# The expert stage of an audio tower: three kinds of transposes in one set, a smaller bias product, and two reorderings beside it

## The chip, the cores and the metric

One core of a Trainium2 chip. The metric is the device time of one execution in microseconds (us). The kernel before was timed in three runs: 778.6, 780.52 and 781.25 us, median 780.52. A profiled execution beside them took 779.15 us.

## The reference, cut to what matters

The whole network has three stages on an input of 32 sequences of 250 positions: a token stage (a recurrence), an attention stage, and a mixture of experts. The change is in the third, which is, on h of shape (32, 250, 64):

```python
x = layernorm(h)
gate_logits = x @ gate_w + gate_b                 # 16 experts
topk_vals, topk_idx = top_k(gate_logits, 2)
topk_w = softmax(topk_vals)
h1 = relu(einsum('bsh,ehf->bsef', x, w1) + b1)    # f = 128 for each expert
expert_out = einsum('bsef,efh->bseh', h1, w2) + b2
moe = sum(topk_w * expert_out[topk_idx])
y = x + moe
out = h + (layernorm(y) * gamma + beta)
```

Every expert is computed for every token; the two chosen ones are picked by a weight that is zero for the other 14.

## The kernel before, in words

**Tiling.** Two sequences are one pair of 500 tokens (C), held in four chunks of T = 125 tokens (CH = 4). There are 16 pairs (PAIRS). The 16 experts times 128 hidden units are cut into 16 groups g of 128 rows; each row of a group is one expert e and one of R = 8 residues r, in the order (e, r). For a group, `up` multiplies the tokens by w1 into one bank of PSUM, the hidden rows are passed through relu and multiplied by the routing weights (`gated`), and `down` multiplies by w2 and sums over the groups in banks 0 and 1. Products are 64 x 64 quarters of the array, four at a time: rows 0 to 63 and rows 64 to 127 belong to two groups or two banks.

**Slots.** The stage is a pipeline written out by hand. Each engine runs its own list over p = 1, 2, ...; in p, pair p-1 goes through the experts, pair p is routed, pair p+1 is normalised, and pairs p-2 and p-3 are finished. A p has eight slots v = 0 to 7. In slot v TensorE (`slot_c`, line 1439) does `up` of groups 2v and 2v+1 of pair p-1 (line 1381) and `down` of an earlier slot's groups (line 1403). Below, "up 6" is the `up` of slot 6, and the time of a pair is from its up 0 to the next pair's up 0.

**Banks and waits.** Group g uses bank 4 + g mod 4 (`up_bank`). So `up` of slot v waits (`wait_read`) until groups 2v-4 and 2v-3 have been read. Groups 1, 4, 6, 9, 12 and 14 (`ACT_GROUPS`) are read by ScalarE (relu, line 730) and multiplied by GpSimd (`gate_group`, line 490); the other ten are read and multiplied by VectorE alone (`fused`, line 1029).

**TensorE's other work in a pair:** `logits` (slot 0, line 1412), the token transposes of pair p+1 (`tokens_c`, slot 3, line 1420, into bank 2), the bias product (`extra`, slot 3, line 1390: four products of 250 columns with `b2f`, in which b2 is repeated and divided by R), the transposes of the routing weights of pair p (`weights_c`, slot 6, line 1428, into bank 3) and those of the result of pair p-2 (`fold_c`, slot 6, line 1436).

**VectorE** (`group_c`, line 1080) goes through g = 0 to 15. At each g it does `fused` of group g, and then what `GATE_AT` (line 1078) puts there: the steps n = 0 to 17 of the routing (`gate_step`), a chain of small operations, each on 125 x 64 values or fewer, each waiting for the one before: logits plus bias (line 989), maximum (993), comparisons and products (995, 997, 1001, 1004), difference of the two best (1007), the two weights times their masks (1017, 1018), and their sum, spread over the R = 8 residues (1022, 125 x 512 values). Step 17 (line 1022) stands behind group 8.

**ScalarE** (`slot_c`, line 715): the normalised tokens of pair p+1 (`normed`, line 688) in slot 1, y_low and y_high (the two copies of pair p-2's sums, lines 720 and 722) in slot 3, the copy of the token transposes (line 680) in slot 3, two sigmoids (`gate_weights`) in slot 4, the copy of the weight transposes to wb (line 713) in slot 6, and the relus of its six groups.

**GpSimd** (`step_c`, line 513): the scales of the two layernorms (`c_scales`), then for each of its six groups the product relu x wb, with `c_total` (y_low + y_high, line 496) behind the third of them, group 6, and `c_result` behind groups 9 and 12.

Of the kernel before, what the change touches and what calls it, by code (L numbers as in the profile page):

```python
# [48 lines left out]
C_COLS = C_II + D  # L49


def constants():

    c = np.zeros((128, C_COLS), np.float32)
    c[:, C_IDENT:C_IDENT + 128] = np.eye(128)

    for half in (0, HALF):
        for part in range(1, PARTS):
            rows = slice(half + part, half + XROWS, PARTS)
            for r in (rows, half + XROWS + part):  # L60
                c[r, C_W1] = -1.0
                c[r, C_W2] = -1.0 if part == 2 else 0.0
    c[64:, C_MS1] = -1.0
    c[Q_ROW + H:Q_ROW + 2 * H, C_MS2] = -1.0
    c[K_ROW + H:K_ROW + 2 * H, C_MS2] = -1.0
    c[:, C_II:C_II + D] = np.tile(np.eye(D), (2, 1))
    for h in range(H):
        c[K_ROW + h, C_IND + h] = 1.0
        c[K_ROW + H + h, C_IND + h] = 1.0
    return c  # L70


def build(nc, cst, xin, xparts, acws, w24, wqT, wkT, wvT, woT, wq, wk, gam, lns,
          gw, gb, w1, b1, w2, b2, fg, fb, out):
    with ExitStack() as ctx:
# [20 lines left out]
        b2raw, b2f = sb("b2raw", [128, D]), sb("b2f", [128, D])  # L96
        fg_sb, fb_sb = sb("fg_sb", [T, D]), sb("fb_sb", [T, D])
# [28 lines left out]
        wtok = sb("wtok", [T, CH, E, R])  # L126
# [45 lines left out]
        s_wprod = sem("s_wprod")  # L172
        a_xin, a_split, a_scr, a_table = sem("a_xin"), sem("a_split"), sem("a_scr"), sem("a_table")
# [91 lines left out]
        def up_bank(g):  # L265
            return bank[4 + g % 4]

# [71 lines left out]
        def _(gp):  # L339
# [173 lines left out]
            def step_c(p):  # L513
                if p < PAIRS + 2:
                    c_scales(p + 1)
                if p == PAIRS:
                    gp.wait_ge(b_res, PAIRS)
                    gp.tensor_tensor(h_fb[:, :, :], h_all[:, (PAIRS - 1) * CH:PAIRS * CH, :],
                                     fb_sb[:, :].unsqueeze(1).to_broadcast([T, CH, D]), ALU.add).then_inc(c_hfb, 1)
                for n, g in enumerate(ACT_GROUPS):  # L520
                    if valid(p - 1):
                        gate_group(p - 1, g)
                    if n == 2 and 0 <= p - 2 < PAIRS - 1:
                        c_total(p - 2)
# [10 lines left out]
        def _(act):  # L535
# [120 lines left out]
            def start_c(v):  # L656

                if v == 0:
                    normed(0)
# [18 lines left out]
            def tokens_c(q):  # L678
                act.wait_ge(c_xt, q + 1)
                act.activation(cs1[q % 3][:, :], bank[2][:, 0:C], ACT.Copy).then_inc(c_s1, 1)  # L680
# [28 lines left out]
            def token_weights(p):  # L709
                act.wait_ge(c_wt, p + 1)  # L710
                wait(act, c_gated, (G - len(ACT_GROUPS)) * (p - 1))
                wait(act, c_gatep, len(ACT_GROUPS) * (p - 1))
                act.activation(wb[p % 2][:, :], bank[3][:, 0:C], ACT.Copy).then_inc(c_wbs, 1)

            def slot_c(p, v):
# [7 lines left out]
                if v == 4 and valid(p):  # L723
                    gate_weights(p)
                for g in (2 * v, 2 * v + 1):
# [6 lines left out]
                if v == 1 and valid(p + 1):  # L732
                    normed(p + 1)
                if v == 5 and 0 <= p - 3 < PAIRS - 1:
                    result(p - 3)
                if v == 3 and valid(p + 1):
                    tokens_c(p + 1)
                if v == 6 and valid(p):
                    token_weights(p)

# [7 lines left out]
        def _(dve):  # L748
# [224 lines left out]
            def gate_step(p, n):  # L973
# [104 lines left out]
            GATE_AT = {2: (0,), 3: (1, 2, 3), 4: (4, 5, 6), 5: (7, 8, 9), 6: (10, 11), 7: (12, 16), 8: (17,)}  # L1078
# [35 lines left out]
        def _(pe):  # L1114
# [234 lines left out]
            def start_c(v):  # L1349

                if v == 1:
                    pe.wait_ge(b_ev, 16 * PAIRS)
                    pe.wait_ge(b_gl, 4 * PAIRS)
                    tokens_c(0)
# [18 lines left out]
            def up(q, v):  # L1373
# [33 lines left out]
            def logits(p):  # L1407
                pe.wait_ge(c_s1, p + 1)
                wait(pe, c_wbs, p)
# [6 lines left out]
            def tokens_c(q):  # L1416
                pe.wait_ge(c_hn, q + 1)
                wait(pe, c_yt, q - 3)
                for c in range(CH):
                    last = pe.transpose(bank[2][:, c * T:(c + 1) * T],  # L1420
# [3 lines left out]
            def weights_c(p):  # L1424
                pe.wait_ge(c_gate, gate_count(p, GATE))
                wait(pe, c_wbs, p)
                for c in range(CH):
                    last = pe.transpose(bank[3][:, c * T:(c + 1) * T],  # L1428
                                        wtok[:, c, :, :].rearrange("p e r -> p (e r)"), ident[0:T, 0:T])
# [9 lines left out]
            def slot_c(p, v):  # L1439
# [104 lines left out]
```

## Time and profile before

| | |
|---|---|
| timed runs | 778.6 to 781.25 us, median 780.52 |
| the profiled execution | 779.15 us, its span 776.6 us |
| TensorE | busy 740.7 us (95% of the span) |
| VectorE | busy 623.8 us (80%) |
| ScalarE | busy 531.5 us (68%) |
| GpSimd | busy 459.4 us (59%) |
| granted TensorE clock | 0.994 of full speed |
| expert stage | from about 498 us to the end |

The expert stage takes about 278 us of the span. Each pair in its middle takes the same time to 0.02 us. The page of the profile gives busy times over the whole span, so the stage has to be read by stretches, and its order by the timeline of each engine.

### The profile page before, as it was taken

The page shows a single profiled execution, that of the slowest core. Times are in us where ns is not written, and L with a number is a line of the kernel's source. Part 1 is how long each engine was busy: PE and PEld are TensorE (multiplying, and loading weights), DVE is VectorE, ACT ScalarE, POOL GpSimd, SP SyncE. Part 2 cuts the span into 40 slices and gives each one's busy share as a digit, 9 for nine tenths or more (in the row PEclk, how much of TensorE's full clock was granted, in tenths as well). Part 3 has the DMA queues.
Part 4 walks back from the last instruction along what each step waited for, and adds up shares of the span by engine and source line. Part 5 has one row for each costly group of instructions (what it writes and reads, how often), then busy time and mean ns, then how long its engine had stood idle before and what let it go on. Part 6 is the DMA issues. An engine that isn't in the chain of part 4 may idle for free.

```text
span 776.6 us, 16767 instructions
## 1 busy us (share of the span) xinstructions
PE 740.7 (95%) x5712; PEld 434.7 (56%) x5712; DVE 623.8 (80%) x1534; ACT 531.5 (68%) x1053; POOL 459.4 (59%) x620
## 2 busy tenths in 40 slices
PE   2999999999999999999999999999999999999994
PEld 1444356676667666676666766444555555454431
DVE  7676777888878888788878887788888888888864
ACT  1566779888888889888898888654555655545441
POOL 7654324654456444564446541366788787888885
PEclk9999999999999999999999999999999999999997
DMA  6300202111221112211221112000000000000000
GB/s 188 94 2 2 55 1 56 35 38 40 55 56 28 42 42 56 53 31 34 51 56 34 37 41 54 2 2 1 9 15 8 9 8 8 9 16 7 9 7 20
DMA packets 22619, 25.46 MB, mean 33 GB/s; under 512 B 12520, under 2 KB 21480, under 8 KB 22408
## 3 DMA queue, kind: packets, MB, share of 16 engines
q1 hardware_dynamic: 21544, 23.14, 12.8%
q10 hardware_dynamic: 992, 1.26, 0.6%
q8 instruction: 46, 0.75, 0.4%
q14 instruction: 37, 0.30, 0.1%
HBM read 5.06 MB, written 2.43 MB: 10 GB/s over the span
## 4 chain that ended last, share of the span: by engine, by line
PE 75%; DVE 10%; DMA 4%; POOL 4%; ACT 3%; issue 3%; SPq 1%; ACTq 0%; DVEq 0%; POOLq 0%
PE bank L1403 14%; PE bank L1381 13%; PE bank L1274 11%; PE bank L1232 9%; PE bank L1298 7%; PE bank L1145 5%; PE bank L1300 5%; DVE m L863 3%; DVE prob L909 3%; DMA m<-s2o 2%; DMA m<-s2e 2%; PE bank L1135 2%; SPq L319 1%; PE bank L1428 1%; PE bank L1236 1%
## 5 line engine op out<-in xcount | busy, mean ns | idle before, releaser
L444 POOL TENSOR_TENSOR sq<-sq 125x256 f32<-125x256 f32 x128 | 98.0, 777 | 187.1 <-ACT sq L596 164.4
L909 DVE TENSOR_SCALAR prob<-prob,cap_hi,cap_lo 125x500 f32<-125x500 f32 x256 | 149.1, 610 | 41.7 <-ACT prob L632 38.7
L632 ACT ACTIVATE prob<-bank 125x500 f32<-125x500 f32 x256 | 148.4, 591 | 33.9 <-PE bank L1300 31.6
L1381 PE MATMUL bank<-cs,w_sb 64*64 64x500 f32 x1024 | 147.0, 580 | 2.2 <-DVE gated L1029 2.0
L1403 PE MATMUL bank<-gated,w_sb 64*64 64x500 f32 x1024 | 148.8, 588 | 0.0
L490 POOL TENSOR_TENSOR gated<-relu,wb 128x500 f32<-128x500 f32 x96 | 120.0, 1251 | 48.1 <-ACT relu L730 45.6
L1029 DVE SCALAR_TENSOR_TENSOR gated<-bank,nb,wb 128x500 f32<-128x500 f32 x160 | 114.8, 727 | 35.2 <-PE bank L1381 35.2
L730 ACT ACTIVATE relu<-bank,b_sb 128x500 f32<-128x500 f32 x96 | 64.7, 674 | 93.2 <-PE bank L1381 93.2
L1381 PEld LDWEIGHTS bank<-cs,w_sb 64*64 64x64 f32 x1024 | 53.1, 133 | 54.7 <-issue 48.1
L596 ACT ACTIVATE sq<-bank 125x512 f32<-125x512 f32 x128 | 75.3, 600 | 4.8 <-POOL sq L444 1.6
L1232 PE MATMUL bank<-wqku_hi,s 128*125 128x512 f32 x192 | 77.2, 402 | 0.0
L1232 PE MATMUL bank<-wqku_lo,s 128*125 128x512 f32 x192 | 75.7, 394 | 0.0
L1403 PEld LDWEIGHTS bank<-gated,w_sb 64*64 64x64 f32 x1024 | 47.0, 132 | 45.0 <-issue 38.3
L1274 PE MATMUL bank<-prob,ue 125*64 125x250 f32 x512 | 61.0, 380 | 0.0
L1274 PE MATMUL bank<-prob,uo 125*64 125x250 f32 x512 | 61.0, 380 | 0.0
L1298 PE MATMUL bank<-m1o,s 128*125 128x500 f32 x128 | 55.4, 433 | 3.3 <-DMA m<-s2o 2.3
L1145 PE MATMUL bank<-st_a,w_sb 64*64 64x500 f32 x224 | 57.8, 588 | 0.0
L1298 PE MATMUL bank<-m1e,s 128*125 128x500 f32 x128 | 55.2, 431 | 2.6 <-DMA m<-s2e 1.6
L1145 PE MATMUL bank<-st_b,w_sb 64*64 64x500 f32 x224 | 57.3, 588 | 0.0
L553 ACT ACTIVATE st_a<-bank 128x500 f32<-128x500 f32 x56 | 32.2, 589 | 32.7 <-PE bank L1145 22.7
L801 DVE TENSOR_SCALAR st_b<-bank 128x500 f32<-128x500 f32 x56 | 37.3, 677 | 20.3 <-PE bank L1145 19.7
L863 DVE TENSOR_TENSOR m<-bank,m1o 64x500 fp32r<-64x500 f32 x64 | 43.2, 675 | 12.5 <-ACT m1o L591 11.8
(188 smaller groups left out, 1572.7 us busy)
## 6 DMA issues: line engine op xcount, KB each, us to landing
m1e<-m1e SPq DMA_DIRECT2D x64, 125.0 KB, 2.3
m1o<-m1o SPq DMA_DIRECT2D x64, 125.0 KB, 2.3
out<-res SPq DMA_DIRECT2D x15, 125.0 KB
w_sb<-in_w SPq DMA_DIRECT2D x1, 1024.0 KB
xa<-xparts SPq DMA_DIRECT2D x3, 281.2 KB
w_sb<-in_w SPq DMA_DIRECT2D x1, 512.0 KB
xw<-xparts SPq DMA_DIRECT2D x3, 140.6 KB
xparts<-x_part SPq DMA_DIRECT2D x3, 125.0 KB, 3.5
```

Of the source, the lines that this page charges most:

```text
L444: gp.tensor_tensor(sq2[q][:, :, :], sq[q][:, :, 0:D // 2], sq[q][:, :, D // 2:D], ALU.add)\
L490: gp.tensor_tensor(gated[g % 8][:, :], relu_sb[n % 3][:, :], wb[q % 2][:, :], ALU.mult).then_inc(c_gatep, 1)
L596: act.activation(sq[k % 2][:, :, :], src[0:T, :].rearrange("p (h d) -> p h d", h=H), ACT.Square)\
L632: act.activation(prob[v % PROBS][:, :, c, :], bank[5 + n % 3][0:T, 0:C].rearrange("p (h l) -> p h l", h=2), ACT.Exp).then_inc(b_exp, 1)
L909: dve.tensor_scalar(part, part, cap_hi[0:T, h:h + 1], cap_lo[0:T, h:h + 1], ALU.min, ALU.max)\
L1029: dve.scalar_tensor_tensor(gated[g % 8][:, :], up_bank(g)[:, 0:C], nb1[:, g:g + 1], wb[q % 2][:, :], ALU.max, ALU.mult).then_inc(c_gated, 1)
L1145: last = pe.matmul(dst[cols, 0:C].rearrange("p (b l) -> p b l", b=2), w24_sb[rows, 0, :], src[rows, :, 0:L], start=False, stop=True)
L1232: last = pe.matmul(dst[0:T, :], s1[j][:, c * T:(c + 1) * T], w[:, q, :], start=first, stop=not first)
L1274: last = pe.matmul(bank[1][64 * c:64 * c + 64, 0:L], u_sb[jj][:, 2 * b + c, h * D:(h + 1) * D], prob[v % PROBS][:, hh, c, :], start=h == 0 ...
L1298: pe.matmul(ps, s1[o][:, cols], m1[o][:, 2 * hp:2 * hp + 2, b * L:(b + 1) * L], start=True, stop=False)
L1381: last = pe.matmul(up_bank(g)[cols, 0:C], w1_sb[rows, g, cols], cs1[q % 3][rows, :], start=True, stop=True)
L1403: last = pe.matmul(y[cols, 0:C], w2_sb[rows, g, :], gated[g % 8][rows, :], start=v == 0, stop=v == 7, skip_group_check=True)
```

## The change

- **One set.** `tokens_c(p+1)` moves from TensorE's slot 3 to slot 6, between `weights_c(p)` and `fold_c(p-2)`. On ScalarE the copy of the tokens follows from slot 3 to slot 6.
- **Banks.** The weight transposes go to bank 6, which is the `up` bank of groups 10 and 14, and wait until group 10 has been read; `up` of slot 7 waits until they have been copied. The token transposes go to bank 3.
- **Step 17 of the routing** (line 1022) moves from behind group 8 to behind step 16, ahead of `fused` of group 8. The sum is laid out as (r, e) in place of (e, r), and w1, b1, w2 are reordered on the host to match.
- **Bias product.** b2 is summed over the residues once (one small product into bank 4 and one copy, in the last attention step), so that each of the four products needs only its own 125 tokens.
- **Two orders.** `normed(p+1)` moves on ScalarE from slot 1 to slot 4, behind the sigmoids and ahead of the relu of group 9. `c_total` moves on GpSimd from behind group 6 to behind group 9.

```diff
-C_COLS = C_II + D
+C_SUM = C_II + D
+C_COLS = C_SUM + 128
...
+    for half in (0, HALF):
+        c[:, C_SUM + half:C_SUM + half + E] = np.tile(np.eye(E), (R, 1))
...
+        def tokens_bank(q):
+            return bank[2 if q < 2 else 3]
+
+        def weights_bank(p):
+            return bank[3] if p == 0 else up_bank(14)
...
-                    if n == 2 and 0 <= p - 2 < PAIRS - 1:
+                    if n == 3 and 0 <= p - 2 < PAIRS - 1:
                         c_total(p - 2)
...
+                if v == 2:
+                    act.wait_ge(c_bsum, 1)
+                    act.activation(b2s[:, :], bank[4][:, 0:D], ACT.Copy).then_inc(c_bias, 1)
...
                 if v == 4 and valid(p):
                     gate_weights(p)
+                if v == 4 and valid(p + 1):
+                    normed(p + 1)
                 for g in (2 * v, 2 * v + 1):
...
-                if v == 1 and valid(p + 1):
-                    normed(p + 1)
...
-                if v == 3 and valid(p + 1):
-                    tokens_c(p + 1)
                 if v == 6 and valid(p):
                     token_weights(p)
+                if v == 6 and valid(p + 1):
+                    tokens_c(p + 1)
...
-                    first, second = (lg[:, k, :, :].unsqueeze(3).to_broadcast([T, CH, E, R]) for k in (5, 6))
+                    first, second = (lg[:, k, :, :].unsqueeze(2).to_broadcast([T, CH, R, E]) for k in (5, 6))
...
-            GATE_AT = {2: (0,), 3: (1, 2, 3), 4: (4, 5, 6), 5: (7, 8, 9), 6: (10, 11), 7: (12, 16), 8: (17,)}
+            GATE_AT = {2: (0,), 3: (1, 2, 3), 4: (4, 5, 6), 5: (7, 8, 9), 6: (10, 11), 7: (12, 16, 17)}
...
+                    pe.matmul(bank[4][:, 0:D], c_sb[:, C_SUM:C_SUM + 128], b2f[:, :], start=True, stop=True)\
+                        .then_inc(c_bsum, 1)
...
+                if v == 7 and valid(q + 1):
+                    pe.wait_ge(c_wbs, q + 2)
...
-                for cols, part in ((LO, slice(0, L)), (HI, slice(L, C))):
-                    for rows, y in ((LO, bank[0]), (HI, bank[1])):
-                        pe.matmul(y[cols, part], b2f[rows, :], wb[q % 2][rows, part], start=False, stop=False,
-                                  skip_group_check=True)
+                for c, (cols, rows, y) in enumerate(((LO, LO, bank[0]), (HI, LO, bank[0]), (LO, HI, bank[1]), (HI, HI, bank[1]))):
+                    part = slice(c * T, (c + 1) * T)
+                    pe.matmul(y[cols, part], b2s[rows, :], wb[q % 2][rows, part], start=False, stop=False,
+                              skip_group_check=True)
...
             def tokens_c(q):
                 pe.wait_ge(c_hn, q + 1)
-                wait(pe, c_yt, q - 3)
+                if q >= 2:
+                    pe.wait_ge(c_gate, gate_count(q - 1, 1))
...
             def weights_c(p):
                 pe.wait_ge(c_gate, gate_count(p, GATE))
                 wait(pe, c_wbs, p)
+                if p > 0:
+                    wait_read(pe, p - 1, 10)
...
             def fold_c(q):
                 pe.wait_ge(c_y, q + 1)
-                pe.wait_ge(c_s1, min(q + 4, PAIRS))
+                pe.wait_ge(c_s1, 2)
+                wait(pe, c_yt, q)
...
-                if v == 3:
-                    if valid(p + 1):
-                        tokens_c(p + 1)
                 if v == 6:
                     if valid(p):
                         weights_c(p)
+                    if valid(p + 1):
+                        tokens_c(p + 1)
                     if valid(p - 2):
                         fold_c(p - 2)
```

## Rows read from the trace of the kernel before

**Rows 1.** Stretches: length, busy PE, PEld, DVE, ACT, POOL, granted clock, DMA, GB/s
```profile
548.00:713.00 165.00, 164.98 (x1644) 83.26 (x1640) 144.39 (x438) 88.89 (x200) 133.97 (x141) 1.00 0.04 10
```

**Rows 2.** Timeline of TensorE, one pair (start us, us, engine, line, operation)
```profile
596.69 1.02 PE L1381 MATMUL bank<-cs,w_sb 64*64 64x500 f32 x8
...
602.10 1.08 PE L1381 MATMUL bank<-cs,w_sb 64*64 64x500 f32 x8
603.11 0.65 PE L1420 MATMUL bank<-c_sb,cxn 125*128 125x125 f32 x4
603.69 1.40 PE L1403 MATMUL bank<-gated,w_sb 64*64 64x500 f32 x8
...
608.35 1.34 PE L1381 MATMUL bank<-cs,w_sb 64*64 64x500 f32 x8
...
613.21 1.02 PE L1381 MATMUL bank<-cs,w_sb 64*64 64x500 f32 x8
```

**Rows 3.** Timeline of VectorE, the same pair
```profile
599.92 0.74 DVE L1029 SCALAR_TENSOR_TENSOR gated<-bank,nb,wb 128x500 f32<-128x500 f32 x1 [1.08 <-PE bank L1381]
...
601.60 0.50 DVE L995 TENSOR_TENSOR lg<-lg,top 125x64 f32<-125x64 f32 x1
...
602.64 0.22 DVE L1001 TENSOR_TENSOR lg<-lg,top 125x64 f32<-125x64 f32 x1
...
603.93 0.45 DVE L1007 TENSOR_TENSOR top<-top 125x4 f32<-125x4 f32 x1
...
606.00 1.17 DVE L1017 TENSOR_TENSOR lg<-lg,top 125x64 f32<-125x64 f32 x1
...
607.23 0.73 DVE L1029 SCALAR_TENSOR_TENSOR gated<-bank,nb,wb 128x500 f32<-128x500 f32 x1
607.88 1.08 DVE L1022 TENSOR_TENSOR wtok<-lg 125x512 f32<-125x512 f32 x1
```

**Rows 4.** Timeline of GpSimd, the same pair
```profile
603.11 1.25 POOL L490 TENSOR_TENSOR gated<-relu,wb 128x500 f32<-128x500 f32 x1 [1.10 <-ACT relu L730]
...
605.85 1.24 POOL L496 TENSOR_TENSOR y_moe<-y_low,y_high 128x500 f32<-128x500 f32 x1
```

**Rows 5.** Timeline of ScalarE, the same pair
```profile
600.83 1.65 ACT L688 ACTIVATE cxn<-h_all,cnb,cinv 125x128 f32<-125x128 f32 x4 [2.37 <-POOL cnb L482]
```

**Rows 6.** Timeline of VectorE in p = 15, which normalises no further pair
```profile
732.29 0.74 DVE L1029 SCALAR_TENSOR_TENSOR gated<-bank,nb,wb 128x500 f32<-128x500 f32 x1 [1.07 <-PE bank L1381]
...
734.94 1.10 DVE L1001 TENSOR_TENSOR lg<-lg,top 125x64 f32<-125x64 f32 x1
...
737.95 1.16 DVE L997 TENSOR_TENSOR lg<-lg,desc 125x64 f32<-125x64 f32 x1
...
739.92 0.46 DVE L1001 TENSOR_TENSOR lg<-lg,top 125x64 f32<-125x64 f32 x1
740.41 0.77 DVE L1017 TENSOR_TENSOR lg<-lg,top 125x64 f32<-125x64 f32 x1
...
741.89 0.68 DVE L1022 TENSOR_TENSOR wtok<-lg 125x512 f32<-125x512 f32 x1
```

**Rows 7.** Timeline of GpSimd in p = 15
```profile
734.72 1.24 POOL L490 TENSOR_TENSOR gated<-relu,wb 128x500 f32<-128x500 f32 x1 [0.40 <-ACT relu L730]
...
737.71 1.31 POOL L496 TENSOR_TENSOR y_moe<-y_low,y_high 128x500 f32<-128x500 f32 x1
```

**Rows 8.** Timeline of TensorE in p = 15
```profile
729.06 1.02 PE L1381 MATMUL bank<-cs,w_sb 64*64 64x500 f32 x8
...
740.15 1.07 PE L1381 MATMUL bank<-cs,w_sb 64*64 64x500 f32 x8 [1.08 <-DVE gated L1029]
...
742.02 1.07 PE L1381 MATMUL bank<-cs,w_sb 64*64 64x500 f32 x8
...
746.60 1.02 PE L1381 MATMUL bank<-cs,w_sb 64*64 64x500 f32 x8
```

**Rows 9.** DMA issues of the first 30 us: KB, us to landing
```profile
c_sb<-in_cst ACTq DMA_DIRECT2D x1, 102.0 KB, 3.2
```

More of the change, by code:

```diff
@@ L96, in build @@
         b2raw, b2f = sb("b2raw", [128, D]), sb("b2f", [128, D])
+        b2s = sb("b2s", [128, D])
         fg_sb, fb_sb = sb("fg_sb", [T, D]), sb("fb_sb", [T, D])
@@ L125, in build @@
         desc = sb("desc", [T, E])
-        wtok = sb("wtok", [T, CH, E, R])
+        wtok = sb("wtok", [T, CH, R, E])
         cagg, cvar = sb("cagg", [T, 2, CH, 2]), sb("cvar", [T, 2, CH])
@@ L172, in build @@
         s_wprod = sem("s_wprod")
+        c_bsum, c_bias = sem("c_bsum"), sem("c_bias")
         a_xin, a_split, a_scr, a_table = sem("a_xin"), sem("a_split"), sem("a_scr"), sem("a_table")
@@ L679, in tokens_c @@
                 act.wait_ge(c_xt, q + 1)
-                act.activation(cs1[q % 3][:, :], bank[2][:, 0:C], ACT.Copy).then_inc(c_s1, 1)
+                act.activation(cs1[q % 3][:, :], tokens_bank(q)[:, 0:C], ACT.Copy).then_inc(c_s1, 1)
             def normed(q):
@@ L712, in token_weights @@
                 wait(act, c_gatep, len(ACT_GROUPS) * (p - 1))
-                act.activation(wb[p % 2][:, :], bank[3][:, 0:C], ACT.Copy).then_inc(c_wbs, 1)
+                act.activation(wb[p % 2][:, :], weights_bank(p)[:, 0:C], ACT.Copy).then_inc(c_wbs, 1)
             def slot_c(p, v):
@@ L1353, in start_c @@
                     pe.wait_ge(b_gl, 4 * PAIRS)
+                    pe.matmul(bank[4][:, 0:D], c_sb[:, C_SUM:C_SUM + 128], b2f[:, :], start=True, stop=True)\
+                        .then_inc(c_bsum, 1)
+                    pe.wait_ge(b_gl, 4 * PAIRS)
                     tokens_c(0)
@@ L1387, in extra @@
                 pe.wait_ge(c_wbs, q + 1)
-                for cols, part in ((LO, slice(0, L)), (HI, slice(L, C))):
-                    for rows, y in ((LO, bank[0]), (HI, bank[1])):
-                        pe.matmul(y[cols, part], b2f[rows, :], wb[q % 2][rows, part], start=False, stop=False,
-                                  skip_group_check=True)
+                if q == 0:
+                    pe.wait_ge(c_bias, 1)
+                for c, (cols, rows, y) in enumerate(((LO, LO, bank[0]), (HI, LO, bank[0]), (LO, HI, bank[1]), (HI, HI, bank[1]))):
+                    part = slice(c * T, (c + 1) * T)
+                    pe.matmul(y[cols, part], b2s[rows, :], wb[q % 2][rows, part], start=False, stop=False,
+                              skip_group_check=True)
             def down(q, v):
@@ L1408, in logits @@
                 pe.wait_ge(c_s1, p + 1)
-                wait(pe, c_wbs, p)
+                if p == 1:
+                    pe.wait_ge(c_wbs, 1)
                 for c in range(CH):
@@ L1417, in tokens_c @@
                 pe.wait_ge(c_hn, q + 1)
-                wait(pe, c_yt, q - 3)
+                if q >= 2:
+                    pe.wait_ge(c_gate, gate_count(q - 1, 1))
                 for c in range(CH):
-                    last = pe.transpose(bank[2][:, c * T:(c + 1) * T],
+                    last = pe.transpose(tokens_bank(q)[:, c * T:(c + 1) * T],
                                         cxn[q % 4][:, c, :, :].rearrange("p a d -> p (a d)"), ident[0:T, 0:T])
@@ L1426, in weights_c @@
                 wait(pe, c_wbs, p)
+                if p > 0:
+                    wait_read(pe, p - 1, 10)
                 for c in range(CH):
-                    last = pe.transpose(bank[3][:, c * T:(c + 1) * T],
-                                        wtok[:, c, :, :].rearrange("p e r -> p (e r)"), ident[0:T, 0:T])
+                    last = pe.transpose(weights_bank(p)[:, c * T:(c + 1) * T],
+                                        wtok[:, c, :, :].rearrange("p r e -> p (r e)"), ident[0:T, 0:T])
                 last.then_inc(c_wt, 1)
@@ L1508 @@
     oT = a("L0_attn_W_o").reshape(D, H, D).transpose(2, 1, 0)
-    w1 = a("L0_ffn_w1").reshape(E, D, G, R)
+    w1 = a("L0_ffn_w1").reshape(E, D, G, R).transpose(1, 2, 3, 0).reshape(D, G, 128)
     arrays = {
@@ L1525 @@
         "gb": rows(a("L0_ffn_gate_b"), T),
-        "w1": np.tile(w1.transpose(1, 2, 0, 3).reshape(D, G, 128), (2, 1, 1)),
-        "b1": a("L0_ffn_b1").reshape(E, G, R).transpose(0, 2, 1).reshape(128, G),
-        "w2": a("L0_ffn_w2").reshape(E, G, R, D).transpose(0, 2, 1, 3).reshape(128, G, D),
-        "b2": np.repeat(a("L0_ffn_b2"), R, axis=0),
+        "w1": np.tile(w1, (2, 1, 1)),
+        "b1": a("L0_ffn_b1").reshape(E, G, R).transpose(2, 0, 1).reshape(128, G),
+        "w2": a("L0_ffn_w2").reshape(E, G, R, D).transpose(2, 0, 1, 3).reshape(128, G, D),
+        "b2": np.tile(a("L0_ffn_b2"), (R, 1)),
         "fg": rows(a("L0_ffn_gamma"), T),
```

## The prediction

> **What bounds the kernel now.** I read the stage by stretches first. In the middle of the expert stage TensorE is busy 164.98 of 165 us at full granted clock [rows 1], while VectorE has 144.39. So TensorE sets the pace there, and one pair takes 613.21 - 596.69 = 16.52 us [rows 2]. The chain of waits says the same: it runs through TensorE for the whole stretch. Next I asked how near the other engines are, because the change rearranges all of them. The reader should look for the point at which TensorE needs something of VectorE. That is up 6, at 608.35 [rows 2], which overwrites the banks of groups 8 and 9 and needs `fused` of group 8 done. VectorE's list from `fused` of group 2 (it starts at 599.92, having waited 1.08 for TensorE) to the end of `fused` of group 8 (607.23 + 0.73 = 607.96) is 8.04 us without a gap [rows 3]. It is done 0.39 before up 6. So there is a second loop, hidden under TensorE by only 0.39 us a pair: VectorE's list from group 2 to group 8, then TensorE from up 6 to the next pair's up 1, which releases the next group 2.
>
> **What makes VectorE's list long.** Some small operations take far longer than their size. L1017 has 125x64 values and takes 1.17, and L1001 of the same size takes 0.22 [rows 3]. L1017 starts at 606.00 and ends at 607.17, and GpSimd's y_moe runs from 605.85 to 607.09 [rows 4]. L1007 (0.45) ends at 604.38, GpSimd's product of group 4 at 604.36. An operation of VectorE with two inputs in SBUF thus stands still until the GpSimd instruction that began before it has ended; `fused`, which reads PSUM, does not (607.23 takes its usual 0.73). The Trainium skill, SBUF — State Buffer, section "Who interferes with whom", states this as an exclusive lock for such pairs, held by whoever issues first; the trace agrees with it, L1017 ending 0.08 after y_moe. So it matters which of the two begins first, and the change moves both.
>
> **The pair in which the new order can be seen.** In p = 15 there is no further pair to normalise and no tokens to transpose in slot 3. In the changed kernel `normed` is gone from slot 1 and the tokens from slot 3 in every p. What ScalarE does there now is 1.65 us of `normed` at 600.83, waiting for GpSimd's scales, with the relu of group 4 queued behind it [rows 5]; GpSimd's product of group 4 then starts 603.11 - 596.69 = 6.42 after up 0 [rows 4], when L1001 (602.64, that is 5.95) is through [rows 3]. In p = 15 the relu is not held, the product starts 734.72 - 729.06 = 5.66 after up 0 [rows 7], 0.22 ahead of L1001 (734.94, that is 5.88), and L1001 takes 1.10 [rows 6]. TensorE stands 1.08 us for `fused` of group 7 at 740.15, and the pair takes 746.60 - 729.06 = 17.54 [rows 8], though it has less work.
>
> **The change part by part.**
> - *One set.* From up 3 (602.10) to the next product (603.69) are 1.59 us [rows 2]. Less the 0.84 of an `up` (16 of them and the smaller work make a pair) and an estimated 0.45 for four transposes (above 0.58, the 603.11 to 603.69 of them, it can't be; below a third of the 0.65 shown it hardly is), 0.30 is the change of the array from quarters to the whole and back, saved once a pair. The transposes themselves are not saved: their 0.45 moves to slot 6.
> - *Bias product.* A group's 500 columns take 0.84, so 250 take 0.42 and 125 take 0.21: saved between 0 (if the number of instructions, which stays, were the limit) and 0.21; I take 0.21.
> - These two are worth 0.51 a pair if TensorE stays the bound. They lie between up 3 and up 4, which is outside TensorE's part of the second loop. If that loop is the bound they save nothing.
> - *Step 17 ahead of group 8* puts L1022 into the second loop: 0.68 unheld [rows 6], 1.08 held [rows 3]. It now stands at the point where GpSimd is idle, waiting for the relu of group 9, which `normed` (1.65) holds back. I take 0.68; bounds 0.68 and 0.68 + 1.24. The other layout of its sum has as many values and costs nothing.
> - *`normed` to slot 4.* It waits for nothing there. Queued behind it are the relu of group 9 (needed by up 6 and by down 4), the relu of group 12 and the copies of slot 6. The relu of group 9 comes some 11.1 after up 0 and up 6 later, so nothing, unless VectorE's list gets short. Its leaving slot 1 is what releases the relu of group 4.
> - *`c_total` behind group 9.* y_moe then no longer stands in front of L1017 (0.95 saved against today) or L997. The fold needs it; it ends near 13.6 and the fold starts near 13.8. Nothing, with little to spare.
> - *Weights by way of bank 6.* They wait for group 10, which VectorE has two operations after group 8, while up 6 runs (0.84): nothing. Up 7 waits for the copy wb; two more sets of transposes and a `down` lie between (1.8 us), against 0.6 for the copy: nothing.
> - *At the ends.* One small product and one copy, once, in attention's last step: 0.1. Constants are 128 columns longer than the 102 KB that land in 3.2 [rows 9], under GpSimd's clearing of memory: 0, above 0.3 without that cover.
>
> **The sum.** VectorE's list as in p = 15: from 732.29 to 0.08 after L1022's start, where `fused` of group 8 ends (as 607.96 to 607.88): 741.97, that is 9.68. Three of its holds go, since y_moe and group 9 now come later: L997 1.16 to 0.22 (y_moe at 737.71 [rows 7]), L1001 0.46 to 0.22, L1017 0.77 to 0.22: 1.73 less. L1022 comes in: 0.68 more. That is 8.63, against 8.04 today. Then 0.10 until up 6 starts (it started 0.05 after), 746.60 - 742.02 = 4.58 to the next up 0 [rows 8], 0.45 for the tokens now in that set, and 3.23 from up 0 to `fused` of group 2 (599.92 - 596.69, and 732.29 - 729.06). Sum 16.99, against 16.52 now: 0.47 more a pair. TensorE's own work would be 16.52 - 0.51 = 16.01; it waits about 1 us a pair.
> Thirteen pairs (p = 2 to 14): +6.1. p = 1 has the same list with more of the routing of its own: between 0 and +0.9, I take +0.5. In p = 15 no `normed` holds back the relu of group 9, so group 9 and y_moe fall on L1001 and L1017 ahead of up 6: 8.63 + 0.95 + 0.95, and L1018 about 0.5 more, is 11.0 against 9.68: +1.4, bounds -0.9 (no hold) and +1.9. p = 16: -0.2. Ends +0.1. Together +7.9: the profiled execution's 779.15 becomes 787.0, and the median, which was 1.4 above it, 788.4. Errors of 0.3 a pair either way give 784 to 793.
>
> **The rivals.**
> *TensorE stays the bound (faster).* The place is GpSimd's group 4 against L1001. If the product starts after L1001, its 0.88 is gone, L1007 comes ahead of group 6, and the list is at most 7.7; TensorE holds the pace once it is under 16.01 - 0.10 - 4.58 - 0.45 - 3.23 = 7.65. Then 14 pairs save 0.51, p = 15 falls from 17.54 by some 1.9: 780.5 - 7.1 - 1.9 - 0.2, about 771. For it speaks a margin of only 0.22 us; against it, that p = 15 shows this order with the same work ahead of it. The Trainium skill, TensorEngine Tiling (Array Packing), section "Key Properties", says that a change of tiling mode drains TensorE, so fewer changes must pay; the rows give 0.30 each, and that decides nothing while VectorE is the bound. Chance 0.12.
> *No difference.* The list comes to 8.16, where the loop is 16.52: half of the holds fall out. 778.2 to 782.8. Chance 0.06.
> *More holds.* The product of group 9 gets ahead of L1022, or L1017, in every pair: that takes 0.65 us of a margin, and costs another 1 us in 13 pairs: about 801. Chance 0.06.
> *The bias product does not shrink.* It changes nothing in the forecast and 3 us in the first rival.
>
> **How the numbers follow.** The forecast has 0.76 and its own range is 784 to 793. Down to 780 it takes in the case without difference and partial holds; the far cases, 771 and 801, are left out, less than 2 in 10 with it. 0.3% (2.3 us) is about what a measurement of this kernel can tell from no change. Faster 0.13, within it 0.05, slower 0.82.
>
> **What would show it.** In the profile after: a pair of 16.9 to 17.1 with L1001 near 0.9 to 1.1 at its first place and L1007 near 0.7; L1017 and L1022 at 0.21 and 0.68; TensorE waiting for `fused` before up 4, up 5 and up 6, about 1 us in all, where it waited for nothing; one set of 12 transposes; the bias product at half its time. It is wrong if L1001 keeps its 0.22, or if TensorE has no idle time in the middle of the stage.

## The result, and the profile after

The changed kernel takes 788.89 us (median of five runs, 787.37 to 789.38) against 780.52 before: the ratio is 1.0103, with a 95% interval of 1.0089 to 1.0116. The forecast was 788.4. The profiled execution took 787.37 us, its span is 785.0 (before: 776.6). Two executions in the experiments below (934 and 1485 us, of the two kernels with two sets, whose other executions lie between 776 and 784) are far off the rest, and the ratios leave them out.

Where the 8.4 us lie can be read from the starts of `logits`, one per pair (worked out from the timeline of TensorE):

| part of the span, us | before | after | difference | forecast |
|---|---|---|---|---|
| start to the first `logits` | 484.63 | 485.34 | +0.7 | +0.1 |
| p = 0 | 14.95 | 14.94 | 0 | 0 |
| p = 1 | 15.58 | 16.07 | +0.5 | +0.5 |
| p = 2 to 14, thirteen pairs | 214.73 | 220.67 | +5.9 | +6.1 |
| p = 15 to the end | 46.66 | 47.93 | +1.3 | +1.2 |

The line numbers have moved: `up` is now L1400, `down` L1424, the bias product L1411, `fused` L1043, the product of GpSimd L501, y_moe L507; the steps L1001, L1007, L1017 and L1022 are L1015, L1021, L1031 and L1036.

First the stretch of [rows 1] in the changed kernel, same columns:

```profile
548.00:713.00 165.00, 162.93 (x1604) 72.96 (x1600) 136.32 (x427) 86.95 (x193) 125.65 (x137) 1.00 0.04 10
```

TensorE still looks full: 162.93 of 165 us. The idle 2.07 us would be 0.2 us in each of the stretch's 9.7 pairs, though a pair is 0.44 us longer with less work in it. Ends of matmuls are modelled, so a short wait between two groups hardly shows in a busy share. The starts show it. One pair of TensorE, to set beside [rows 2]:

```profile
600.39 1.02 PE L1400 MATMUL bank<-cs,w_sb 64*64 64x500 f32 x8
...
605.80 1.08 PE L1400 MATMUL bank<-cs,w_sb 64*64 64x500 f32 x8
606.86 1.44 PE L1424 MATMUL bank<-gated,w_sb 64*64 64x500 f32 x7
...
608.43 1.07 PE L1400 MATMUL bank<-cs,w_sb 64*64 64x500 f32 x8
609.29 1.05 PE L1424 MATMUL bank<-gated,w_sb 64*64 64x500 f32 x8
610.55 1.07 PE L1400 MATMUL bank<-cs,w_sb 64*64 64x500 f32 x8 [0.21 <-DVE gated L1043]
...
612.35 1.07 PE L1400 MATMUL bank<-cs,w_sb 64*64 64x500 f32 x8
...
617.36 1.02 PE L1400 MATMUL bank<-cs,w_sb 64*64 64x500 f32 x8
```

The pair takes 617.36 - 600.39 = 16.97. Up 5 (610.55) starts 2.12 after up 4, where an `up` and a `down` are 1.68; up 6 (612.35) starts 1.80 after up 5; up 4 starts 1.57 after down 0 (606.86), where a `down` and the smaller bias product are 1.05. That is 1.08 us of gaps, all before the three `up`s that were named. The bracket shows 0.21 of it. They cost 0.71 net: the pair takes 16.26 in the version below in which VectorE is out of the way. The other 0.37 is lost in that version too, in another form. The half of down 0 that writes bank 1 starts 0.39 behind the half that writes bank 0. With gaps the late half catches up in them; without, it stays late until the transposes (down 0 to up 6 takes 4.66 there, where the products are 4.41, and up 6 to the transposes 1.12 in place of 1.00).

VectorE and GpSimd in the same pair, to set beside [rows 3, 4]:

```profile
603.62 0.74 DVE L1043 SCALAR_TENSOR_TENSOR gated<-bank,nb,wb 128x500 f32<-128x500 f32 x1 [1.07 <-PE bank L1400]
...
606.33 1.05 DVE L1015 TENSOR_TENSOR lg<-lg,top 125x64 f32<-125x64 f32 x1
...
608.44 0.66 DVE L1021 TENSOR_TENSOR top<-top 125x4 f32<-125x4 f32 x1
...
610.56 0.22 DVE L1031 TENSOR_TENSOR lg<-lg,top 125x64 f32<-125x64 f32 x1
...
610.96 0.69 DVE L1036 TENSOR_TENSOR wtok<-lg 125x512 f32<-125x512 f32 x1
611.57 2.02 DVE L1043 SCALAR_TENSOR_TENSOR gated<-bank,nb,wb 128x500 f32<-128x500 f32 x3
...
606.05 1.25 POOL L501 TENSOR_TENSOR gated<-relu,wb 128x500 f32<-128x500 f32 x1 [0.35 <-ACT relu L746]
607.84 1.25 POOL L501 TENSOR_TENSOR gated<-relu,wb 128x500 f32<-128x500 f32 x1 [0.55 <-ACT relu L746]
611.62 1.25 POOL L501 TENSOR_TENSOR gated<-relu,wb 128x500 f32<-128x500 f32 x1 [2.53 <-ACT relu L746]
```

GpSimd's product of group 4 begins at 606.05, 0.28 ahead of L1015, and L1015 ends 0.08 after it (606.33 + 1.05 against 606.05 + 1.25). L1021 runs against group 6 (607.84). L1031 and L1036 are free, because group 9 comes at 611.62 and y_moe behind it. From `fused` of group 2 to the end of `fused` of group 8 (611.57 + 0.73) are 8.68 us.

### The profile page after: what moved, and what is told of

It is laid out like the page before. It is cut to its first block, busy times and chain, and to the rows that moved or that the text cites. A ratio compares the mean times of both kernels' runs of the same rounds, so it can differ in the third digit from the quotient of the medians.

```text
span 785.0 us, 16762 instructions
## 1 busy us (share of the span) xinstructions
PE 744.7 (95%) x5714; PEld 425.2 (54%) x5714; DVE 620.0 (79%) x1534; ACT 533.5 (68%) x1054; POOL 453.8 (58%) x620
## 4 chain that ended last, share of the span: by engine, by line
PE 62%; DVE 20%; DMA 6%; issue 5%; ACT 3%; POOL 3%; SPq 1%; ACTq 0%; DVEq 0%; POOLq 0%
PE bank L1288 11%; PE bank L1400 9%; PE bank L1246 9%; PE bank L1312 7%; PE bank L1424 7%; PE bank L1159 5%; PE bank L1314 5%; DVE gated L1043 4%; DVE m L877 3%; DVE prob L923 3%; DMA m<-s2o 2%; DVE lg L1015 2%; DMA m<-s2e 2%; PE bank L1149 2%; SPq L330 1%
## 5 line engine op out<-in xcount | busy, mean ns | idle before, releaser
L501 POOL TENSOR_TENSOR gated<-relu,wb 128x500 f32<-128x500 f32 x96 | 119.7, 1249 | 62.2 <-ACT relu L746 61.4
L1043 DVE SCALAR_TENSOR_TENSOR gated<-bank,nb,wb 128x500 f32<-128x500 f32 x160 | 113.8, 728 | 46.1 <-PE bank L1400 46.1
L1400 PE MATMUL bank<-cs,w_sb 64*64 64x500 f32 x1024 | 136.6, 588 | 6.9 <-DVE gated L1043 6.7
L1424 PE MATMUL bank<-gated,w_sb 64*64 64x500 f32 x1024 | 141.9, 587 | 0.2
L1400 PEld LDWEIGHTS bank<-cs,w_sb 64*64 64x64 f32 x1024 | 41.8, 132 | 69.3 <-issue 50.8
L1424 PEld LDWEIGHTS bank<-gated,w_sb 64*64 64x64 f32 x1024 | 44.7, 132 | 55.8 <-issue 48.0
```

The lines of the kernel that those rows point to most:

```text
L501: gp.tensor_tensor(gated[g % 8][:, :], relu_sb[n % 3][:, :], wb[q % 2][:, :], ALU.mult).then_inc(c_gatep, 1)
L1043: dve.scalar_tensor_tensor(gated[g % 8][:, :], up_bank(g)[:, 0:C], nb1[:, g:g + 1], wb[q % 2][:, :], ALU.max, ALU.mult).then_inc(c_gated, 1)
L1400: last = pe.matmul(up_bank(g)[cols, 0:C], w1_sb[rows, g, cols], cs1[q % 3][rows, :], start=True, stop=True)
L1424: last = pe.matmul(y[cols, 0:C], w2_sb[rows, g, :], gated[g % 8][rows, :], start=v == 0, stop=v == 7, skip_group_check=True)
```

## Experiments

Each is the changed kernel with one edit, unless it says otherwise. A *hold* is the time by which an operation of VectorE with two inputs in SBUF takes longer than usual because a GpSimd instruction that began before it has not ended. The ratio is to the kernel before on the same chip, with its 95% interval; "pair" is the steady distance from one `logits` to the next in the middle of the stage (16.53 before, 16.97 changed).

### Which of the reorderings costs what

**`normed` back to slot 1.**

```diff
-                if v == 4 and valid(p + 1):
-                    normed(p + 1)
...
+                if v == 1 and valid(p + 1):
+                    normed(p + 1)
```

> The changed kernel (788.9 us) with normed back in ScalarE's slot 1, all else kept. Theory A (the pair's time is VectorE's list from group 2 to group 8, and which GpSimd product stands in front of its two-input operations sets that list): the relu of group 4 is held back again, so the first L1015 goes back from 1.05 to 0.22 us; but the relu of group 9 is no longer behind normed, its product begins about 2 us earlier and falls in front of the routing's last steps (L1031, L1036). Laid out with the durations of the trace: a pair of 16.75 in place of 16.97, in all about 2 us less: 787. Rival B (the set of three in slot 6, with weights waiting for group 10 and up 7 for the copy wb, is what makes the pair longer): nothing on that path moves, 16.97 a pair, 789, and the first L1015 does not matter.

Measured: 786.92 us, ratio 1.0067 [1.0043, 1.0091], pair 16.75. The product of group 4 now starts after the first L1015, which falls to 0.22, as the forecast's cause requires. But only 0.22 of the 0.44 us comes back. The expectation had the number, but not the reason: it let the product of group 9 fall on L1031 and L1036, and the product begins at 610.42, when L1036 (609.85, 0.69) has begun and runs free. VectorE's list ends at 611.19, 0.35 ahead of up 6 (611.54), so it no longer sets the pace. A second bound lies right under the first: down 0 waits for y_low, which stands on ScalarE behind `normed` and the relu of group 4. It is read below beside the kernel with two sets.

**`c_total` back behind group 6** (`n == 3` to `n == 2`).

> The changed kernel with c_total (y_moe) back behind GpSimd's group 6. Theory A: y_moe then runs directly behind the product of group 6, in front of L1011 and the steps after it, and everything behind comes under the product of group 9 as well: a pair of about 18.8 in place of 16.97, some 24 us more in all: 813. Rival B (set of three is the cause): y_moe is ready 2 us earlier for the fold, so no change or a gain of up to 0.1 a pair: 787 to 789.

Measured: 812.82 us, ratio 1.0396 [1.0369, 1.0423], pair 18.83. Timeline of VectorE and GpSimd, one pair:

```profile
617.59 1.15 DVE L1011 TENSOR_TENSOR lg<-lg,desc 125x64 f32<-125x64 f32 x1
...
620.20 1.62 DVE L1036 TENSOR_TENSOR wtok<-lg 125x512 f32<-125x512 f32 x1
...
617.36 1.30 POOL L507 TENSOR_TENSOR y_moe<-y_low,y_high 128x500 f32<-128x500 f32 x1
619.93 1.34 POOL L501 TENSOR_TENSOR gated<-relu,wb 128x500 f32<-128x500 f32 x1 [1.28 <-ACT relu L746]
```

y_moe holds L1011 (1.15 for 0.23), that makes VectorE late, and so the product of group 9 now begins 0.27 ahead of L1036 (1.62 for 0.69). Two holds of 0.92 and 0.93 are the whole 1.86 us a pair. One hold breeds the next: this is the largest effect in the study, and no engine has more work.

**Step 17 back behind group 8.**

```diff
-            ... 7: (12, 16, 17)}
+            ... 7: (12, 16), 8: (17,)}
```

> The changed kernel with step 17 (L1036) back behind fused of group 8, as before the change. Theory A with the holds laid out: behind group 8 the step begins only after the product of group 9 has begun and is held by it to its end (about 1.1 to 1.3 in place of 0.69), group 10 is late, and the transposes wait for the step: about 17.3 a pair, 793. Theory A in the simple form of the prediction's sum (0.68 us of VectorE's list is taken out of the loop, and nothing else moves): 16.97 - 0.6 = 16.4 a pair, 781. Rival B: 789 or more, as weights come later.

Measured: 791.37 us, ratio 1.0131 [1.0109, 1.0154], pair 17.36. Step 17 is off VectorE's list before up 6, and still the pair is 0.39 longer. Timeline of VectorE, GpSimd and TensorE, one pair:

```profile
614.16 0.68 DVE L1036 TENSOR_TENSOR wtok<-lg 125x512 f32<-125x512 f32 x1
...
614.29 1.67 POOL L501 TENSOR_TENSOR gated<-relu,wb 128x500 f32<-128x500 f32 x1 [2.53 <-ACT relu L746]
...
617.23 0.70 PE L1462 MATMUL bank<-c_sb,y_moe 128*125 128x128 f32 x4 [0.26 <-POOL y_moe L507]
```

The expectation had the size, but let GpSimd hold VectorE. It is the other way round. VectorE begins first and GpSimd is held: the product of group 9 takes 1.67 instead of 1.25, y_moe behind it is late by as much, and TensorE's fold waits for y_moe. So the moves of step 17 and of `c_total` belong together. With `c_total` behind group 9, GpSimd's order is on the path too.

### The bias product

**The bias product of before, 4 x 250 columns with b2f, in the changed kernel.**

> The changed kernel with the old bias product (four products of 250 columns with b2f). Theory A: it lies between up 3 and up 4, where TensorE waits for fused of group 5 anyway, so 0.0 a pair: 788.9, and TensorE's wait in front of up 4 is 0.2 shorter. Rival C (TensorE's own work still counts in the pair): 0.21 more in each of 16 pairs, 3.3 us: 792.

Measured: 789.02 us, ratio 1.0104 [1.0078, 1.0131], pair 16.97: no difference. The smaller product is worth nothing here.

**The bias product alone, on the kernel before** (with the (r, e) layout that it needs; one set, `normed`, `c_total` and step 17 as before).

> The kernel before (780.6 us, 16.53 a pair) with nothing of the change but the smaller bias product and the (r, e) layout that it needs. Theory C (TensorE is the bound before, 164.98 of 165 us busy, so work taken from it is gained): 0.21 less in 16 pairs, 3.3 us: 777. Theory A (the holds decide, and VectorE's list has only 0.39 us of slack): up 4 and everything behind it comes 0.2 earlier, so the relu and the GpSimd product of group 6 and of group 9 come earlier against VectorE's steps, and steps that were just ahead of them fall under them. Laid out: about 17.0 a pair, 785; with latencies off by 0.02 us it can stay at 16.5 (779), so 779 to 786, and no gain of 3 us.

Measured: 785.58 us, ratio 1.0069 [1.0052, 1.0085], pair 16.98. Work was taken from an engine that was busy 164.98 of 165 us, and the kernel became slower by 0.45 us a pair. The two timelines side by side, VectorE and GpSimd. Before:

```profile
607.09 0.21 DVE L1018 TENSOR_TENSOR lg<-lg,top 125x64 f32<-125x64 f32 x1
...
607.16 1.25 POOL L490 TENSOR_TENSOR gated<-relu,wb 128x500 f32<-128x500 f32 x1
```

With the bias product alone:

```profile
609.40 1.17 DVE L1025 TENSOR_TENSOR lg<-lg,top 125x64 f32<-125x64 f32 x1
610.49 1.28 DVE L1026 TENSOR_TENSOR lg<-lg,top 125x64 f32<-125x64 f32 x1
...
609.25 1.24 POOL L501 TENSOR_TENSOR y_moe<-y_low,y_high 128x500 f32<-128x500 f32 x1
610.45 1.24 POOL L495 TENSOR_TENSOR gated<-relu,wb 128x500 f32<-128x500 f32 x1
```

Before, VectorE's second product (L1018) begins 0.07 us ahead of GpSimd's group 9, which was still waiting for its relu. With TensorE 0.21 us earlier the relu is ready, the product follows y_moe at once, begins 0.04 ahead of L1026, and L1026 takes 1.28 instead of 0.21. That is theory A of the expectation, also in its number. The kernel before was held together by a margin of 0.07 us that no view of busy shares shows.

**Two sets as before, with the smaller bias product, `c_total` behind group 9 and step 17 ahead of group 8** (on the kernel before). This is the changed kernel without the one set and without the move of `normed`.

> The kernel that stands to e1_normed_slot1 (786.9, 16.75 a pair) as two sets to one: token transposes in slot 3 into bank 2, weight transposes in bank 3, their copy in slot 3; all else as in e1 (smaller bias product, step 17 ahead of group 8, c_total behind group 9, normed in slot 1). Theory F (in slot 3 the token transposes cover the time in which down 0 would otherwise wait for ScalarE's y_low and y_high, and their 0.45 us is not in the part of the loop behind up 6): one set costs, it does not save: two sets give 16.37 a pair, and in all about 780. Theory G (what the change says: one change of the array's mode less per pair is gained when the rest is equal): two sets cost 0.3 a pair more than one: 17.05, 791.

Measured: 781.31 us, ratio 1.0009 [0.9994, 1.0023], pair 16.32. That is 16.53 - 0.21: TensorE is the bound again, with exactly the bias product's saving. Against the first experiment (pair 16.75), which differs by the one set alone, the one set costs 0.43 us a pair. Timeline of TensorE with one set (first experiment):

```profile
605.56 1.08 PE L1400 MATMUL bank<-cs,w_sb 64*64 64x500 f32 x8
607.11 1.44 PE L1424 MATMUL bank<-gated,w_sb 64*64 64x500 f32 x8 [0.47 <-ACT y_low L734]
...
611.54 1.41 PE L1400 MATMUL bank<-cs,w_sb 64*64 64x500 f32 x8
...
614.32 1.07 PE L1424 MATMUL bank<-gated,w_sb 64*64 64x500 f32 x8
```

and with two:

```profile
602.44 1.08 PE L1391 MATMUL bank<-cs,w_sb 64*64 64x500 f32 x8
...
604.03 1.39 PE L1415 MATMUL bank<-gated,w_sb 64*64 64x500 f32 x8
...
608.49 1.34 PE L1391 MATMUL bank<-cs,w_sb 64*64 64x500 f32 x8
...
610.78 1.07 PE L1415 MATMUL bank<-gated,w_sb 64*64 64x500 f32 x8
```

From up 3 to down 0 are 1.55 us with one set and 1.59 with two. The transposes are gone from there, but down 0 overwrites banks 0 and 1 and must wait for the copies y_low and y_high; the transposes had filled exactly that wait. From up 6 to down 3 are 2.78 with one set and 2.29 with two: the tokens' 0.49 is really added there. In sum +0.45 by these rows (0.43 by the pairs), and nothing of the change of the array is saved.

The same parts of the span as in the table above, worked out for this kernel, show why it doesn't beat the one before although each of its pairs does: thirteen pairs give 2.7 us, p = 1 takes back 1.0 and p = 15 to the end 2.7. In p = 15 no `normed` delays the relu of group 9, and its product and y_moe hold VectorE in turn. Some 1.5 us of the last 2.7 are of another kind. TensorE stands still for VectorE ahead of up 6 of p = 15:

```profile
742.11 1.94 PE L1391 MATMUL bank<-cs,w_sb 64*64 64x500 f32 x8 [2.31 <-DVE gated L1037]
```

Up 6 takes 1.94 us where it takes 1.07 in the changed kernel (750.57, shown further down, after as long a wait), and up 6 to the next up 0 takes 6.08 against 4.58. The granted clock is 0.50 from 742 to 744 us here (1.2 of 2.4 GHz) and 1.00 throughout p = 15 in the changed kernel. The first experiment's trace has the same fall (granted clock 0.65 from 748 to 750 us and 0.50 from 750 to 752), with p = 15 to the end at 49.5. A wait of 2.3 us in this place was followed by half clock in two of the five traces that have it. The timed executions of this kernel point the same way: with a mean granted clock of 0.995 they took 778.2 to 779.7 us (three), with 0.992 or 0.993 they took 780.2 to 783.3 (eight). By an estimate from the three, this kernel takes 0.5 to 2 us less than the one before where the clock stays up.

### What the hold is made of

**Step 5 with its second input from PSUM** (it reads bank 3 instead of the maxima in SBUF; the token transposes wait for it).

> The changed kernel with step 5 of the routing (the first L1015 of a pair, 1.05 us) taking its second input from PSUM (the logits' bank) in place of SBUF, same size and same place, and the token transposes waiting for it. The comparison then has another right side, so the mask of the best expert, and with it the weights and the output, are not the reference's; the work is the same in amount. Theory A (a VectorE operation with two SBUF inputs stands still under a GpSimd instruction that began first): step 5 takes 0.2 us though the product of group 4 runs at that moment; the next two-input steps and the relu of group 9 move 0.8 earlier and meet the products of groups 6 and 9 instead, so the pair gains little: 16.9 to 17.0, 788 to 789. Rival D (the step is slow for its data or its wait, not for GpSimd): it stays near 1.05. Rival E (holds add up): the pair falls by the whole 0.8: 16.2, 777.

Measured: 786.62 us, ratio 1.0081 [1.0063, 1.01], pair 16.98. Timeline, one pair:

```profile
605.08 0.22 DVE L1015 TENSOR_TENSOR lg<-lg,bank 125x64 f32<-125x64 f32 x1
605.33 0.80 DVE L1021 SCALAR_TENSOR_TENSOR lg<-lg 125x64 f32<-125x64 f32 x1
...
604.80 1.25 POOL L501 TENSOR_TENSOR gated<-relu,wb 128x500 f32<-128x500 f32 x1 [0.35 <-ACT relu L746]
```

With one input from PSUM the same step takes 0.22 in the middle of GpSimd's product, where it took 1.05. So it is the second SBUF input that is held, not the operation. The next step, which has two, then stands until the product's end (0.80, ending 0.08 after it). The hold moves by one instruction, and the pair stays as it is. The time that is gained lies in p = 1, where 15.04 us stand for 16.07.

**The steps of the routing spread ahead of the products.**

```diff
-            GATE_AT = {2: (0,), 3: (1, 2, 3), 4: (4, 5, 6), 5: (7, 8, 9), 6: (10, 11), 7: (12, 16, 17)}
+            GATE_AT = {1: (0, 1, 2, 3), 4: (4, 5), 5: (6,), 6: (7, 8, 9), 7: (10, 11, 12, 16, 17)}
```

> The changed kernel with GATE_AT = {1: (0, 1, 2, 3), 4: (4, 5), 5: (6,), 6: (7, 8, 9), 7: (10, 11, 12, 16, 17)}: four steps are moved ahead of fused of group 2, into the 1.07 us in which VectorE waits for up 1 there. Simple count of VectorE's list: about 1 us shorter, a pair of 16.0, 774. Theory A with the holds laid out: step 2 then meets the 1.66 us power of c_scales on GpSimd (L491, from 2.16 to 3.82 after up 0) and is held until it ends, so fused of group 2 is late: about 17.2 a pair, 791.

Measured: 775.33 us, ratio 0.9942 [0.9923, 0.9962], pair 16.26. Theory A's expectation failed, in sign and by 16 us; the simple count's 774 is near. Timeline of VectorE, GpSimd and TensorE, one pair:

```profile
598.63 0.23 DVE L1009 TENSOR_TENSOR lg<-lg,top 125x64 f32<-125x64 f32 x1
598.89 0.22 DVE L1011 TENSOR_TENSOR lg<-lg,desc 125x64 f32<-125x64 f32 x1
...
598.22 1.66 POOL L491 TENSOR_TENSOR cinv<-cvar,mhalf 125x8 f32<-125x8 f32 x1
...
601.47 1.08 PE L1400 MATMUL bank<-cs,w_sb 64*64 64x500 f32 x8
602.53 1.44 PE L1424 MATMUL bank<-gated,w_sb 64*64 64x500 f32 x7
```

Steps 2 and 3 have two inputs in SBUF and run inside GpSimd's L491 (the power of `c_scales`, 1.66 us on 125x8 values), and neither is held. All 28 such overlaps of steps 2 and 3 in this trace are at 0.22 or 0.23. The expectation had let L491 hold them to its end. VectorE's list from group 2 to group 8 is 7.85 us after that (599.28 to 607.13), in place of 8.68. By the sum of the forecast its loop would take 7.85 + 0.05 + 5.01 + 3.23 = 16.14, less than the 16.26 measured, so VectorE no longer sets the pace, though by only 0.12. The same stretch of the profile shows:

```profile
548.00:713.00 165.00, 165.00 (x1680) 86.01 (x1678) 144.41 (x453) 91.00 (x201) 135.34 (x144) 1.00 0.05 10
```

**The same with `c_scales` behind GpSimd's group 1.**

> As the run before, with c_scales moved on GpSimd behind the product of group 1, so that VectorE's four steps do not meet its 1.66 us power. Theory A with the holds laid out: the steps run while VectorE would wait for up 1, the list from group 2 to 8 fits under TensorE nearly everywhere, 16.2 a pair in place of 16.53 before and 16.97 after: about 775, faster than both. Rival B (set of three is the cause): no gain against after: 789.

Measured: 775.86 us, ratio 0.9946 [0.993, 0.9963], pair 16.26. As L491 holds nothing, moving it gains nothing. One of the thirteen pairs takes 17.29 here, and it shows what a margin is. In the others L1036 begins 0.05 or 0.06 us ahead of GpSimd's product of group 9 and is free (0.69). In this one VectorE is 0.17 us late for a reason that the trace doesn't show, the product begins first (655.28 against 655.39), and L1036 takes 1.68.

**Two sets with the steps moved ahead** (the kernel with two sets above, with this order of the steps).

```diff
+            GATE_AT = {1: (0,), 2: (1,), 3: (2, 3, 4), 4: (5, 6), 5: (7,), 7: (8, 9, 10, 11, 12, 16), 8: (17,)}
```

> As s1_two_sets, with GATE_AT = {1: (0,), 2: (1,), 3: (2, 3, 4), 4: (5, 6), 5: (7,), 7: (8, 9, 10, 11, 12, 16), 8: (17,)}: one step in the wait ahead of group 2, and the two-input steps gathered where GpSimd's products leave room. Theory A with the holds laid out: 16.45 a pair, p = 15 without its 1 us of waiting: 775 to 777, which would make the single set unnecessary for the best time. If the set of three is worth something by itself, this stays above g1_steps_ahead_only (775.3) by more than 3 us: 778 or more.

Measured: 778.1 us, ratio 0.9968 [0.9955, 0.9981], pair 16.44. The pair is as expected (16.45), the time is above the 775 to 777 named. It lies 2.8 us above the one set with the steps spread, just under the 3 that were to tell whether the one set is worth something by itself, and the two differ in the order of the steps too: that stays open. Inside the stage it is 2.9 us shorter than before, 1.3 of it in the thirteen pairs and 1.6 from p = 15 on. Its pair is 0.12 longer than with two sets and the first order of steps: step 17 behind group 8 stretches y_moe from 1.24 to 1.71 (610.19 to 611.90), and the fold starts right behind it, at 611.95.

The fastest version of the study is thus the changed kernel with the steps spread: 775.33 us, 0.58% under the kernel before and 1.7% under the changed one.

## Why the prediction was right

**The loop.** The forecast's sum held term by term: list 8.68 (forecast 8.63), 0.05 until up 6 (0.10), 5.01 from up 6 to the next up 0 (4.58 + 0.45), 3.23 to `fused` of group 2 (3.23): 16.97 against 16.99. The signs that it named are there: 1.05 at the first L1015, 0.66 at L1021, 0.22 and 0.69 at L1031 and L1036, waits before up 4, 5 and 6. Of the 1.08 us of gaps (forecast about 1) only 0.71 count, since TensorE's own pair is 16.26. What made this possible was p = 15 of the kernel before [rows 6 to 8], which showed the new order of events in the old trace.

**p = 1 and p = 15.** The +0.5 of p = 1 is as forecast, but it was the middle of a range from 0 to 0.9, with nothing laid out behind it: luck. p = 15 takes 18.97 us from up 0 to up 0 (forecast 17.54 + 1.4). Timeline of TensorE, VectorE and GpSimd, to set beside [rows 6 to 8]:

```profile
736.18 1.02 PE L1400 MATMUL bank<-cs,w_sb 64*64 64x500 f32 x8
...
750.57 1.07 PE L1400 MATMUL bank<-cs,w_sb 64*64 64x500 f32 x8 [2.31 <-DVE gated L1043]
...
755.15 1.02 PE L1400 MATMUL bank<-cs,w_sb 64*64 64x500 f32 x8
...
746.36 1.16 DVE L1031 TENSOR_TENSOR lg<-lg,top 125x64 f32<-125x64 f32 x1
747.45 1.27 DVE L1032 TENSOR_TENSOR lg<-lg,top 125x64 f32<-125x64 f32 x1
748.75 1.11 DVE L1036 TENSOR_TENSOR wtok<-lg 125x512 f32<-125x512 f32 x1
...
746.11 1.33 POOL L501 TENSOR_TENSOR gated<-relu,wb 128x500 f32<-128x500 f32 x1 [1.23 <-ACT relu L746]
```

The size is right and the places are one later than forecast: group 9, y_moe and the operation behind them fall on L1031, L1032 and L1036 (0.94, 1.05 and 0.42 too long), not on the second L1001 and L1017. (The lower bound given for p = 15, -0.9, should be -1.05 by its own sum, 8.63 against 9.68; nothing rests on it.)

**Ahead of the stage.** Here a term was mis-sized: "ends +0.1" against +0.7. But the change is not what did it. The 0.7 arises near 21 us, where one stretch of the recurrence's products still ran at nearly half the speed; from 22 us on the changed kernel's recurrence is 0.73 behind throughout. TensorE of before and then of after:

```profile
20.76 0.58 PE L1145 MATMUL bank<-st_a,w_sb 64*64 64x500 f32 x1
```

```profile
20.89 1.04 PE L1159 MATMUL bank<-st_b,w_sb 64*64 64x500 f32 x2
```

The first `logits` start between 484.22 and 487.18 us in the twelve profiled executions, and at 484.22 and 484.63 in two that have the same constants and first products as the changed kernel. In the traces of before and of the `c_total` experiment 8 of these products take about 1.04 us, in the changed kernel 16. So this part differs by up to 3 us from one execution to the next, and that the total came within 0.5 us of the forecast is in part chance. The granted clock of the stretch from 20 to 22 us is 1.00 in both traces; what slows the products there is open. Inside the stage the forecast was +7.8 and the measurement +7.7.

**TensorE's own work was too low.** The forecast gave 16.01 us a pair and, in the first rival, 771 us, if VectorE had been fast enough. With VectorE out of the way the pair takes 16.26, not 16.01. The step that failed is the saving of "One set": it counted the change of the array (0.30) as pure gain and took the tokens out of slot 3 at no cost, but they covered down 0's wait for ScalarE's copies. ScalarE in the changed kernel:

```profile
606.13 0.59 ACT L734 ACTIVATE y_low<-bank 128x500 f32<-128x500 f32 x1 [0.16 <-PE bank L1424]
```

It starts as soon as the sums are there and its end, 606.72, is what releases the first half of down 0 at 606.86. Up 3 to down 0 is 1.06 where an `up` is 0.84: 0.22 us of waiting. The half of down 0 that writes bank 1 waits for y_high, the next copy:

```profile
606.61 0.58 ACT L736 ACTIVATE y_high<-bank 128x500 f32<-128x500 f32 x1
```

In every trace, before the change too, that half starts 0.05 us after y_high has ended; it is the 0.39 behind the first half that was named above. So TensorE waited for ScalarE in the kernel before as well, under a busy share of 164.98 of 165. With `normed` in slot 1 the copies are later still, and the same wait is 0.71. The forecast's number didn't depend on it, since VectorE's list was longer; the rival's 771 did.

The Trainium skill, TensorEngine Tiling (Array Packing), section "Key Properties", says that a change of mode drains TensorE. The one set of the changed kernel agrees: up 6 to down 3 takes 2.44 us, and less the 0.84 of an `up` and three times the 0.43 of four transposes (613.83 to 614.26) that leaves 0.31 for the way out and back. The forecast's 0.30 was thus right in size, but the row that it was read from doesn't show it: up 3 to down 0 takes 1.59 with the transposes and 1.55 without. One such way less was worth 0.06 us a pair at best (16.32 with two sets, 16.26 with one, which differ in the order of steps and of `normed` too), because of that wait.

**The cause.** That `normed`'s leaving slot 1 puts GpSimd's product ahead of L1001 is shown: put back, the hold is gone. That it is the only bound is not so; the one set alone already costs 0.43 us a pair. In the order two sets, one set, `normed` moved, the pair is 16.32, 16.75, 16.97. What the one set costs or saves with `normed` in slot 4 was not run. The forecast had the last value and its mechanism, and priced the step before it as a gain.

## What to carry to other kernels

When two engines block each other by turns, list for every pair of their instructions which begins first and by how much; a margin of 0.07 us decided 0.45 us a pair here, and taking work from the busy engine turned it the wrong way. Before moving work off a spot, ask what it covers there. And look for an odd iteration (the last pair, the first) in the old trace: it may already run in the order that the change will bring.

## What the runs showed of the hardware

GpSimd's power operation on 125x8 values takes 1.66 us and doesn't hold VectorE's operations with two inputs in SBUF (0.22 and 0.23 us inside it, 28 times), while its products on 128x500 values do. In the twelve traces 430 operations of VectorE on 125x64 values begin 0.03 to 1.1 us behind such a product or y_moe, and each ends 0.08 or 0.09 us after it; the one on 125x512 values ends 0.55 us after it. A tie can go either way. Of 52 operations on 125x64 values that VectorE begins within 0.02 us of the product or of y_moe, 47 run freely (0.21 or 0.22) and the product takes 1.30 to 1.34; the other five are held and take 1.31. The Trainium skill, SBUF — State Buffer, section "Who interferes with whom", lets whoever issues first hold the pair for the whole instruction. The products agree with it, the power operation doesn't; whether it gives the port back after reading its 8 values a partition was not tried. The section's other statement, that an operation with at most one input in SBUF is not held, agrees with step 5 (0.22 from PSUM, 1.05 from SBUF).

The hold works both ways: a VectorE operation of 0.68 us that began 0.13 us earlier stretched GpSimd's product from 1.25 to 1.67 us.

A standing TensorE can cost twice. After 2.31 us without a product ahead of up 6 of p = 15 the granted clock fell to 0.50 (1.2 of 2.4 GHz) in two traces, and up 6 took 1.94 us instead of 1.07; in three others the clock stayed at 1.00 after a wait of 2.31 to 2.35 us. What tells them apart is open.
